# Which transfer opens SyncE's queue, and how many matmuls on zeros run before the first data

## The reference

```python
W = weights[condition]                                  # (64, 64, 64)
y = jnp.einsum('bct,bcd->bdt', x, W)                    # the mix of channels
gate_logits = jnp.einsum('bsd,ed->bse', y, gate_w)      # 8 experts
weights, selected = jax.lax.top_k(gate_logits, 2)       # then a softmax over the two
result = jnp.einsum('bsd,od->bso', y, base_w) + base_b
low = jnp.einsum('bsd,erd->ebsr', y, lora_A)            # rank 16
lora_out = jnp.einsum('ebsr,eor,bse->bso', low, lora_B, w_full)
return x + result + 2.0 * lora_out
```

## Time and profile before

| | us |
|---|---|
| median of 3 runs | 477.17 |
| lowest and highest | 476.44, 477.21 |
| the profiled execution, its own time | 476.71 |
| its span, first to last instruction | 474.9 |
| TensorE busy in the span | 470.1 |

### The profile page before, as it was taken

How to read it: one execution, slowest core, us unless ns; L and a number is a source line. 1 busy time by engine, 2 the same in 40 slices (tenths; PEclk the granted TensorE clock), 3 DMA queues, 4 the chain that set the end, 5 groups by cost and what they waited for, 6 DMA issues and landing times.

```text
span 474.9 us, 8144 instructions
## 1 busy us (share of the span) xinstructions
PE 470.1 (99%) x2660; PEld 461.7 (97%) x2660; DVE 352.4 (74%) x636; ACT 158.9 (33%) x262; POOL 116.8 (25%) x113
## 2 busy tenths in 40 slices
PE   8999999999999999999999999999999999999997
PEld 8999999999999999999999999999999999999996
DVE  3967969897786967858687686867869587685843
ACT  4733444224233412333223333422333223432300
POOL 2345142040411404123041420414124041310400
PEclk9999999999999999999999999999999999999999
DMA  8966523626265262733625355262743625344202
GB/s 318 413 229 217 194 95 132 226 68 244 86 203 175 115 213 66 248 111 148 222 92 179 110 188 187 90 230 55 245 130 134 221 87 202 112 169 121 90 23 88
DMA packets 49275, 76.91 MB, mean 162 GB/s; under 512 B 13666, under 2 KB 32226, under 8 KB 49250
## 3 DMA queue, kind: packets, MB, share of 16 engines
q1 hardware_dynamic: 37586, 71.88, 43.2%
q10 hardware_dynamic: 11664, 4.72, 3.7%
HBM read 41.98 MB, written 34.60 MB: 161 GB/s over the span
## 4 chain that ended last, share of the span: by engine, by line
PE 99%; DVE 0%; ACT 0%; issue 0%; POOL 0%; POOLq 0%
PE acc L911 50%; PE acc L903 29%; PE acc L949 9%; PE mixed L943 9%; PE acc L1106 1%; PE acc L929 0%; PE mixed L929 0%; DVE y_lo L614 0%; ACT y_hi L467 0%; DVE x_sb L896 0%; POOL y_moved L360 0%; POOLq L1153 0%
## 5 line engine op out<-in xcount | busy, mean ns | idle before, releaser
L386 POOL TENSOR_TENSOR x_sb<-x_sb,bias 128x1024 f32<-128x1024 f32 x32 | 77.1, 2428 | 220.8 <-DVE x_sb L747 181.5
L903 PE MATMUL acc<-r_hi,y_lo 128*128 128x392 f32 x256 | 87.0, 340 | 0.2 <-DVE y_lo L614 0.2
L903 PE MATMUL acc<-r_hi,y_hi 128*128 128x392 f32 x256 | 86.9, 339 | 0.0
L903 PE MATMUL acc<-r_lo,y_hi 128*128 128x392 f32 x256 | 86.6, 339 | 0.0
L911 PE MATMUL acc<-t_lo,s_hi 128*128 128x384 f32 x224 | 74.9, 334 | 0.0
L911 PE MATMUL acc<-t_hi,s_lo 128*128 128x384 f32 x224 | 74.8, 334 | 0.0
L911 PE MATMUL acc<-t_hi,s_hi 128*128 128x384 f32 x224 | 74.8, 334 | 0.0
L911 PE MATMUL acc<-t_lo,y_hi 128*128 128x384 f32 x216 | 72.4, 335 | 0.0
L911 PE MATMUL acc<-t_hi,y_lo 128*128 128x384 f32 x216 | 72.3, 335 | 0.0
L911 PE MATMUL acc<-t_hi,y_hi 128*128 128x384 f32 x216 | 72.2, 334 | 0.0
L655 DVE TENSOR_TENSOR y_lo<-y_turned,y_hi 128x512 fp32r<-128x512 f32 x60 | 46.0, 807 | 24.3 <-ACT y_hi L523 24.1
(11 more groups left out here) (81 smaller groups left out, 744.6 us busy)
## 6 DMA issues: line engine op xcount, KB each, us to landing
x_sb<-in_x SPq DMA_DIRECT2D x32, 512.0 KB, 4.7
out<-x_sb SPq DMA_DIRECT2D x31, 512.0 KB, 3.1
y_scratch<-y_whole SPq DMA_DIRECT2D x60, 256.0 KB, 2.1
y_moved<-y_scratch SPq DMA_DIRECT2D x120, 128.0 KB, 2.8
t_raw<-in_w_quads SPq DMA_DIRECT2D x4, 768.0 KB, 9.2
scratch<-low_turns ACTq DMA_DIRECT2D x16, 128.0 KB, 1.8
low_turns<-scratch ACTq DMA_DIRECT2D x64, 32.0 KB, 2.4
r_raw<-in_w_plain SPq DMA_DIRECT2D x8, 196.0 KB, 5.1
```

The source lines that it names most:

```text
L386: nc.gpsimd.tensor_tensor(x_sb[:, slot(c), :], x_sb[:, slot(c), :], bias[:, :], ALU.add) \
L903: return nc.tensor.matmul(acc[:, i, 0:NP], y_part[:, i, k, :], w_part[:, k, :], start=(k == 0 and product == 0), stop=(k == KT - 1 and pro ...
```

## The change

The transfer of the list of conditions leaves SyncE's queue, where it was the first, and is issued by GpSimd, between its first and second memset. The first pair of x becomes the first transfer of SyncE's queue. TensorE runs ten matmuls on zeros where it ran twelve. Nothing else is changed, and the rest of the program, all 16 steps, keeps its order.

```diff
@@ -270,7 +270,7 @@
         LOOPS = (STEPS - 7) // 3
         LAST = STEPS - 1
-        WARM = 12
+        WARM = 10
         MOVES = QUARTERS
@@ -282,7 +282,6 @@
             def load_quad(i, room):
                 sp.dma_start(room, w_quads[i]).then_inc(quad_in[i], 16)
 
-            sp.dma_start(cond_sb[:, :], condition).then_inc(cond_in, 16)
             sp.dma_start(first_x[:, 0, :], x_first_pairs[0]).then_inc(first_in[0], 16)
             for k in range(KT):
                 sp.dma_start(r_raw[:, k, :], w_plain[k]).then_inc(r_in[k], 16)
@@ -358,6 +357,7 @@
         @block.gpsimd
         def _(pool):
             nc.gpsimd.memset(zeros, 0.0).then_inc(zeros_ready, 1)
+            pool.dma_start(cond_sb[:, :], condition).then_inc(cond_in, 16)
             nc.gpsimd.memset(w_pair, 0.0).then_inc(w_zero, 1)
             nc.gpsimd.memset(earlier[:, :, :], 0.0).then_inc(ident_zero, 1)
             pool.wait_ge(ident_zero, 1)
```

## The result

The changed kernel took 480.75 us (median of 4 runs, 480.37 to 481.00) against 477.0 before on the same chip; the ratio is 1.0083, with a 95% interval of 1.0069 to 1.0097. The prediction was 477.1 with a range to 478.2, so it was wrong, and on the slower side. The profiled execution took 480.49 with a span of 478.7, 1.8 us outside the span as before. All 3.8 us are inside it.

What follows compares the result with a forecast made beforehand. It took TensorE, busy 99% of the span, as the bound. Zeros -0.84, waits for x and cw +0.76, slow clock +0.03, conditions 0 made about -0.05 on the median 477.17: 477.1 us, range 476.3 to 478.2.

Steps and rivals of the forecast that it cites:

- What bounds the kernel now: Whole kernel: TensorE busy 99% of the span; at the 6.13 hand-over the zeros end last, x next at 5.7.
- the microsecond of room: Behind the opening: the second pair's y_lo ends at 14.1, needed about 15.1, so 0.05 to 0.3 us gained passes through.
- x first: SyncE's queue: x issued 0.40 us earlier; later landing of x and cw at 5.6, cw last, hand-over about 6.05.
- The conditions: List on GpSimd's queue: issued at 1.0, landing 2.2 to 4.6, taken as 3.2; cost 0.
- The way from the list to the mix: After the list lands: 1.4 us for GpSimd's reads and register work, then 0.42 for the copy of cw.
- Rival B: Opening: the list lands after 4.2 and becomes last, giving 477.4 to 478.1; chance 0.17 shared with D.
- Rival C: Opening: TensorE's idle time delays the clock's rise, slowing mix and first products, +1.4 to +1.7, 478.7; chance 0.11.
- D: GpSimd's first transfer costs engine or launch something no row shows; range 477.4 to 478.1, chance 0.17 shared with Rival B.
- The zeros: Before the mix: two matmuls on zeros fewer, four instructions, -0.84 us, with +0.76 given back to waits for x and cw.

Runs made afterwards that it cites:

- the second of the changed kernel: The changed kernel run once more, unaltered, beside the kernel before on the same chip: 480.78 us, 4.48 over before.
- the one with 26: The changed kernel with 26 matmuls on zeros instead of ten: 479.48 us, 3.10 over the kernel before.
- without the list: The changed kernel with fixed matrices for the first two pairs, so nobody waits for the list at the start: 477.02 us.
- x second: The kernel before, twelve matmuls kept, with the list by GpSimd's queue and a spare 256-byte transfer ahead of x on SyncE's queue: 479.54 us.
- the list by SyncE: The changed kernel with the list issued on SyncE's queue behind x and two pieces of r_raw, instead of by GpSimd: 481.43 us.

## Why the prediction was wrong

**What bounds the kernel now: right.** The zeros, x and `cw` were read as they are, with x at 5.7; ten matmuls on the kernel before moved the hand-over to 5.81, near the 5.7 of the prediction. Nothing behind the opening changed; the microsecond of room and more was there, even for a shift of 3.8.

**x first: the mechanism right, the size not.** The prediction said that the stream of 1.0 MB sets the end, not the issue, that `cw` would be last and that the gain would vanish. `cw` was last. But the bounds of 5.3 to 5.7 for the later landing left out that two queues served side by side could be slower than one after the other. The later of them landed at 5.6 in two of the traces (the second of the changed kernel, the one with 26) and at 6.4 to 6.5 in the other four in which they were issued together. From 2 to 4 us the engines moved 0.45 MB in the changed kernel's trace (47 packets of `cw`, 64 of x) where 0.58 MB had passed in the earlier trace rows; in its second trace, with the landing at 5.6, 0.57 MB. So side by side they are slower in some executions and not in others, and why is open. The hand-over without the list was at 6.81, not 6.05: +0.5 us in the time, not -0.05. The Trainium skill ("DMA: Bandwidth & Descriptors", Issuing engines are not separate DMA queues) says that transfers of several issuing engines interleave, and this time the trace agrees (47 packets and 64).

**The conditions: the step that failed.** "That is 2.2 to 4.6. I take 3.2." The list took 5.55 us from 1.35, and landed at 6.90. The upper bound was the nearest large transfer, 512 KB in 3.6 us, on the thought that 256 bytes cannot take longer than those. They can, because they stand behind two of them. The earlier trace rows had shown the very thing: x, issued by 1.57, hardly moved until `cw` was nearly done (22 packets of its queue to 135 of `cw` from 2 to 4 us). The prediction read that row for x and not for the list. Applied to the list, it puts the first packet where x and `cw` are nearly through; in the traces with the two side by side that was 5.1 to 5.4, and the first read of the list 6.4 to 6.9. The guess of 1.0 for the issue was also short: the engine began it at 1.35. The Trainium skill's figure for the first byte of a GpSimd transfer ("DMA: Bandwidth & Descriptors", Latency and other measured facts) gave an estimate of 2.6 in the prediction, for an issue at 1.0. With no other traffic the trace is not far from it (1.38 + 1.8 = 3.2 for the landing, issued 0.4 later); behind x and `cw` the estimate misses by about 4 us (6.4 to 6.9).

**The way from the list to the mix: right in kind, short by 0.25.** 1.4 for reads and 0.42 for a copy were forecast; from 6.90 to 8.97 it took 2.07, since VectorE's first copy, from 8.66, ends a little behind GpSimd's, from 8.51, and TensorE needs both.

**The slower side: both rivals came, and together.** Rival B (the list last) had the right mechanism with a range that ended at 478.1, because its landing ended at 5.5. Rival C (the clock) forecast +1.4 to +1.7; alone it is +1.3, with four matmuls on zeros. It had 0.11 because the prediction set it against a pause of 0.35 to 0.8 us, and there it does not decide: pauses of 0.9, 1.1 and 1.6 us left the mix fast. It needed the list's lateness to make a pause of 2.8 to 3.3 us. Treated as cases that exclude each other, B (with D) and C got 0.28 between them and no range that held their sum, 476.3 + 0.5 + 2.6 + 1.4 = 480.8.

**The zeros.** -0.84, all given back, as forecast. In the changed kernel they count for nothing on either side: twelve gave 480.86, ten 480.78.

## What to carry to other kernels

A tiny transfer that gates everything should be issued ahead of the large ones, first on its queue: it was in 1.2 to 1.7 us after its issue here (2.0 to 2.5 on the clock of the trace), against 4.3 to 5.5 us when it was issued behind 1 MB. What did not help was a queue of its own for a transfer issued later than the large ones. Before bounding a transfer's latency, ask what will be on the engines when its packets come, and read that from the row where another small or late transfer already stood behind a large one. And where matmuls on zeros bridge a wait to keep the clock up, a longer wait and a colder clock are one case, not two: price them together.

## What the hardware showed that was not expected

- A 256-byte load by GpSimd's queue took 1.8 and 1.7 us from issue to landing with no other traffic, 4.3 to 4.5 behind `cw` and x issued one after the other, 5.1 to 5.5 behind the two issued together; GpSimd was held by the issue for 0.64 us.
- Two 512 KB loads issued at 0.80 and 0.81 us on two queues had both ended at 5.6 to 6.5; with `cw` issued first and x 0.4 us behind, at 4.4 and 5.7; with x first and `cw` 0.55 us behind, at 4.2 and 6.3.
- After pauses of 2.44 us (x second) to 4.50 us (the list by SyncE) TensorE did all or most of the mix at the lower level of its clock, 3.50 to 3.78 us for 16 instructions; after pauses of 0.57 to 1.60 us, and after none, in the variants it took 1.95 to 2.05. In the trace of the list by SyncE the zeros ended at 5.10, and the granted clock was 1.00 up to 7.7 and 0.50 from 7.75, with TensorE idle all the time. The moment at which the clock first rises differed between executions of kernels with nearly the same opening: the zeros took 0.21 us each throughout the changed kernel's two traces, but 20 of them took 3.85 us in the kernel before with ten.
